# Attention's layer normalisation, in a two-layer decoder on one core: VectorE's apply step becomes a GpSimd shift and a ScalarE ACTIVATE

## The reference

```python
def _layernorm(x, axis=-1, eps=1e-05):
    m = jnp.mean(x, axis=axis, keepdims=True)
    v = jnp.var(x, axis=axis, keepdims=True)
    return (x - m) / jnp.sqrt(v + eps)
...
    x = _layernorm(x + _L0_attn_ref(x, ...), axis=-1)                 # a long convolution
    x = _layernorm(x + _L0_xattn_ref(x, ctx_1024, ...), axis=-1)      # cross attention, 16 heads of 32
    x = _layernorm(x + _L0_ffn_ref(x, ...), axis=-1)
    x = _layernorm(x + _L1_attn_ref(x, ...), axis=-1)                 # retention
    x = _layernorm(x + _L1_xattn_ref(x, ctx_1024, mask, ...), axis=-1)  # cross attention, masked
    x = _layernorm(x + _L1_ffn_ref(x, ...), axis=-1)
```

```python
        scores = jnp.einsum('bhqd,bhkd->bhqk', q, k) / scale
        attn = jax.nn.softmax(scores, axis=-1)
        out = jnp.einsum('bhqk,bhkd->bhqd', attn, v)
        return out @ Wo + bo
```

## Time and profile before

| | |
|---|---|
| median of 3 runs | 2520.98 us (2520.63 to 2522.58) |
| the profiled execution, its own time | 2518.09 us |
| its span, first to last instruction | 2516.3 us |
| mean granted TensorE clock | 0.902 |
| TensorE busy | 2193.9 us, 87% |
| VectorE busy | 1147.9 us, 46% |
| ScalarE busy | 946.2 us, 38% |
| GpSimd busy | 761.2 us, 30% |

### The profile page before, as it was taken

The page is one execution under the profiler, slowest core; times in us unless marked ns, Lnnn a source line. Parts: engine busy times, 40 slices in busy tenths (PEclk is TensorE's granted clock), DMA queues, the critical chain, the costliest instruction groups (busy, mean ns, idle before and its releaser), DMA issues.

```text
span 2516.3 us, 36343 instructions
## 1 busy us (share of the span) xinstructions
PE 2193.9 (87%) x12528; PEld 2014.5 (80%) x12528; DVE 1147.9 (46%) x1742; ACT 946.2 (38%) x1603; POOL 761.2 (30%) x554
## 2 busy tenths in 40 slices
PE   4798889888866889689988889879999999999997
PEld 3687778777755777578777778769999999999996
DVE  7456666566556268446566665554620001100022
ACT  2354545454442244345444545442222223211131
POOL 4333232233243633422133222222222222222222
PEclk9798899898867978789988999869999999999998
DMA  4354455344321100255354454321111121112111
GB/s 152 109 152 111 123 139 138 100 127 127 117 70 30 34 11 0 86 174 146 102 137 112 120 143 134 92 80 46 66 51 59 58 64 61 51 58 67 58 50 43
DMA packets 126422, 226.33 MB, mean 90 GB/s; under 512 B 39896, under 2 KB 77016, under 8 KB 126232
## 3 DMA queue, kind: packets, MB, share of 16 engines
q1 hardware_dynamic: 126360, 225.52, 30.9%
HBM read 169.93 MB, written 55.53 MB: 90 GB/s over the span
## 4 chain that ended last, share of the span: by engine, by line
PE 75%; DVE 10%; issue 6%; POOL 4%; ACT 3%; DMA 1%; SPq 1%; DVEq 0%; POOLq 0%; ACTq 0%
PE psS L310 13%; PE psS L312 12%; PE psS L311 12%; PE psO L1607 6%; PE psJ L310 4%; PE psS L1564 4%; PE psJ L311 4%; PE psJ L312 4%; PE psT L1593 3%; PE psT L310 3%; DVE psS L1129 2%; PE psT L311 2%; PE psT L312 2%; PE psS L1593 2%; DVE x_res L1083 2%
## 5 line engine op out<-in xcount | busy, mean ns | idle before, releaser
L310 PE MATMUL psS<-hid_hi,fw_hi 128*128 128x400 f32 x1152 | 397.9, 345 | 15.3 <-DVE hid_lo L1490 10.6
L312 PE MATMUL psS<-hid_hi,fw_lo 128*128 128x400 f32 x1152 | 400.0, 347 | 0.0
L311 PE MATMUL psS<-hid_lo,fw_hi 128*128 128x400 f32 x1152 | 399.4, 347 | 0.0
L690 POOL TENSOR_TENSOR fw_lo<-raw,fw_hi 128x1024 fp32r<-128x1024 f32 x88 | 216.6, 2461 | 572.5 <-ACT fw_hi L947 572.5
L513 POOL TENSOR_TENSOR pT<-p,pT 128x600 fp32r<-128x600 f32 x112 | 164.9, 1473 | 656.7 <-ACT pT L775 656.7
L1129 DVE TENSOR_REDUCE psS<-psS 100x1 f32<-100x722 f32 x256 | 234.6, 916 | 195.8 <-PE psS L1564 195.4
L1490 DVE TENSOR_TENSOR hid_lo<-h_act,hid_hi 128x800 fp32r<-128x800 f32 x32 | 32.3, 1082 | 555.7 <-ACT hid_hi L1039 555.7
L1564 PE MATMUL psS<-kS,qS 97*100 97x512 f32 (+1 forms) x512 | 165.6, 391 | 119.4 <-DVE psS L1129 81.1
L310 PE MATMUL psJ<-cT_hi,wk_hi 128*128 128x362 f32 (+1 forms) x512 | 189.9, 371 | 62.6 <-POOL cT_lo L506 36.1
L310 PEld LDWEIGHTS psS<-hid_hi,fw_hi 128*128 128x128 f32 x1152 | 217.9, 189 | 16.3 <-issue 11.3
L312 PEld LDWEIGHTS psS<-hid_hi,fw_lo 128*128 128x128 f32 x1152 | 219.2, 190 | 0.0
(11 more groups left out here) (315 smaller groups left out, 4677.6 us busy)
## 6 DMA issues: line engine op xcount, KB each, us to landing
kS<-k_parts SPq DMA_DIRECT2D x384, 180.5 KB
raw<-ffn_dram SPq DMA_DIRECT2D x88, 512.0 KB, 3.5
k_parts<-kst SPq DMA_DIRECT2D x64, 362.0 KB, 3.2
k_parts<-kst SPq DMA_DIRECT2D x64, 360.0 KB, 2.8
ctx_raw<-ctxT_dram SPq DMA_DIRECT2D x32, 361.0 KB, 3.8
ctx_late<-ctxT_dram SPq DMA_DIRECT2D x28, 361.0 KB, 3.8
qS<-q_parts SPq DMA_DIRECT2D x192, 50.0 KB, 2.2
q_parts<-qst SPq DMA_DIRECT2D x16, 400.0 KB, 2.6
```

Of the source, the lines that this page charges most:

```text
L310: nc.tensor.matmul(out, st[0], mv_[0], start=first, stop=False)
L311: nc.tensor.matmul(out, st[0], mv_[1], start=False, stop=False)
L312: return nc.tensor.matmul(out, st[1], mv_[0], start=False, stop=last)
L690: nc.gpsimd.tensor_tensor(fw.lo[:, e, :], raw[:, e, :], fw.hi[:, e, :], ALU.subtract)\
```

## The change

In the 7 batches of each attention layer that follow another one, the apply step of pair 3 is no longer VectorE's. GpSimd computes the shift, -mean x rstd, into `veps`, directly behind the root in pair 1 (`shift`). ScalarE writes x_res = rstd x y + shift with one ACTIVATE (`norm_apply` in its own block), in pair 3, behind the copy of the maxima, and tells `ln_x`. It waits for a new semaphore `A.shift`. The normalisation of each layer's last batch stays on VectorE, and so do all others.

```diff
+            def shift(L, b):
+
+                n = (LN_ATT0, LN_ATT1)[L] + b
+                wait_apart(pool, ln_rstd, n + 1)
+                nc.gpsimd.tensor_scalar(veps[:, 0, :], mv[:, 0, 0:1], rstd[:, 0, :], -1.0, ALU.mult, ALU.mult)\
+                  .then_inc(A.shift, 1)
...
                         if t == 1 and not first:
                             root(base + b - 1, 0)
+                            shift(L, b - 1)
...
+                def norm_apply(b):
+
+                    act.wait_ge(A.shift, b + (NB - 1) * L + 1)
+                    nc.scalar.activation(x_res[:, b, :], y[:, 0, :], ACT.Identity, bias=veps[:, 0, :],
+                                         scale=rstd[:, 0, :]).then_inc(ln_x, 1)
...
-                def batch(b, last):
+                def batch(b, last, first=False):
...
                         if t == 2 and not last:
                             context_hi(L, b + 1, 0)
+                        if t == 3 and not first:
+                            norm_apply(b - 1)
...
-                batch(0, False)
+                batch(0, False, first=True)
...
                         if t == 4:
                             low_parts(b, 2 * t + 1)
-                        if t == 3 and not first:
-                            norm_apply(base + b - 1, 0, y[:, 0, :], b - 1)
```

More of the change, by code:

```diff
@@ L259, in decoder_kernel @@
                          "q_mm q_hi q_lo q_out0 q_out1 qs_in0 qs_in1 qs_in2 qs_in3 s_mm maxed nm_hi nm t_mm rows_set st_mm exped pt_hi lo_even lo_odd pv_mm "
-                         "u_done sums r_done z_done x_done o_sum o_scaled o_biased o_hi o_lo resid_done mask_in mask_done "
+                         "u_done sums r_done z_done x_done o_sum o_scaled o_biased o_hi o_lo resid_done mask_in mask_done shift "
                          "mask_out pads")
```

## The result

| | us |
|---|---|
| before, median of 4 runs beside the change | 2521.2 (2520.63 to 2522.58) |
| after, median of 4 runs | 2432.97 (2430.58 to 2437.87) |
| ratio, 95% interval | 0.9652 (0.9635 to 0.9668) |
| after, profiled execution: own time, span, granted clock | 2434.05, 2432.3, 0.921 |

A forecast was written before the change was run, and what follows sets the result against it. TensorE bounds the kernel, waiting while VectorE's normalisation stands still until GpSimd's run ends. Loops 77.3 less ScalarE's 1.2 gives 76.1 us off 2518.09, 2442; plus 2.9 for the median, 2445 us; range 2429 to 2464.

The forecast's parts named there:

- The loops, 77.3 us: Twelve attention loop cycles, freed of VectorE's held normalisation, fall from 913.85 to 836.6 us.
- The mean of two controls: Each layer's first batch, with no previous batch to normalise, took 69.03 and 70.40 us; 69.7 forecast per loop cycle.
- ScalarE, 0.77 us with 0.1 to spare, a charge of 1.2 us: Pair 3's new ACTIVATE takes 0.77 us, fits before head 8's exponential; 0.1 us a batch charged for lateness.
- GpSimd, nothing: The shift behind pair 1's root takes 0.4 us, covered by 2.74 us of idle time, so costs nothing.
- The last batches, nothing: Each layer's last batch splits no context slices, so VectorE is not held long; 0 gain for both.
- The sum: Whole kernel: 76.1 us off the profiled 2518.09 gives 2442 us; 2.9 us added for the median gives 2445.
- A: Attention cycles: TensorE's clock stays low, only the 5.1 us stalls go; gain 61 us, 2460 us; chance 0.09.
- B: Pair 3: ScalarE's ACTIVATE is held 6.6 us beside GpSimd's run; gain 16 us, 2505 us; chance 0.03.
- C: Attention cycles: TensorE settles at the low clock of 0.54, 59 us slower, 2580 us; chance 0.03.
- D: Key projection stays at 453.3 anyhow, no change, chance 0.02; partial form, a new 3 us wait, 2480 us, 0.03.

The follow-up runs named there:

- e1: Kernel before, with the apply step left on VectorE but moved from pair 3 to pair 5, behind the output sums: 2433.98 us, ratio 0.9659.
- e3: Kernel after, plus an unused VectorE maximum over 100x6144 at the step's old place in the twelve loop batches: 2513.05 us, ratio 0.9968.
- e4: Kernel after, with ScalarE's new apply step done twice, the second waiting for the first: 2438.50 us, ratio 0.9680.
- e5: Kernel after, with pair 3's apply step back on VectorE in the two last batches alone: 2439.46 us, ratio 0.9681.
- e2: Kernel before, with the apply step on VectorE at its old place, cut into pieces of 257 and 255 elements: 2519.99 us, ratio 1.0003.
- e7: Kernel after, with context slice 1's low part moved from GpSimd to VectorE in pair 3 of every batch but the last: 2484.76 us, ratio 0.9858.
- e9: Kernel after, plus an unused VectorE reduction over 100x3072 in the twelve loop batches, half of an earlier 100x6144 block: 2468.03 us, ratio 0.9797.

## Why the prediction was right, and where not

- *The loops, 77.3 us.* Measured 79.3. The mechanism is shown three ways: take the step away (after), move it out of the run (e1), put a stall of the same length back (e3).
- *The mean of two controls.* Right, and for a reason I did not have: the cycles fall into the controls' two kinds.
- *ScalarE, 0.77 us with 0.1 to spare, a charge of 1.2 us.* Measured 0.82 and 0.17 to spare, so the charge should have been about nothing. That lateness arrives whole was too strong (e4: two thirds).
- *GpSimd, nothing.* The idle time ahead of the next low probabilities fell from 2.74 to 2.19 us, so the shift cost 0.55 us, all covered. e1 has neither the shift nor the ACTIVATE, and its loops are only 0.3 us shorter.
- *The last batches, nothing.* This is the term that was mis-sized: 6.5 us by e5, 5.4 of it seen in the trace of layer 1's last batch. I looked at how long VectorE is held and at layer 0's 0.54 us, and passed over layer 1, where the step took 1.72 us. What it cost there was hardly the pause, and mostly the clock at which TensorE worked afterwards. In layer 0 nothing came of it: head 8 of its last batch to head 8 of layer 1's first took 454.4 us before and 454.1 after.
- *The sum.* The profiled execution took 2434.05 us where 2442 was worked out. Of these 8 us, 2.0 are the loops, 1.2 the ScalarE charge and 7.2 the end of layer 1, against 2.7 us lost up to head 8 of layer 0's batch 0 and in layer 1's batch 0: 7.7. The other 4 us up to the medians come from the executions: I added 2.9 us because before's median lies above its profiled execution; after's lies 1.1 below it. Why layer 1's batch 0 ran at 0.90 is open. That the time lies in the range is in part luck: the loops as forecast reached down to 2435 us, the rest down to 2429 was meant for loop cycles at a clock of 1.00, which did not come, and what filled it was the end of layer 1, a term put at nothing.
- *Rivals.* A (clock gives nothing back) is out: 0.96 for 0.91. B (the hold moves) is out: 817 ns. C and D are out with the loops' 834.58 us.

## What to carry to other kernels

When a VectorE operation that should take half a microsecond takes several, look whether it ends just as a GpSimd operation, or a whole uninterrupted run of them, ends. If so, move the step to where VectorE has slack, or hold GpSimd back with a wait at the end of a stage: here the first was worth as much as moving the step to another engine (e1). Price a stall by TensorE's cycle around it, not by its own length: a cycle of the same work without the stall is the best estimate, and a pause of 1.3 us cost more than five in one place. After a bound is gone, follow who released the next wait: here VectorE, then GpSimd and ScalarE's cast at once, which had to be moved together.

## What the hardware showed that was not expected

- In the attention loops VectorE was held until GpSimd's run ended, whatever it had left to do: 6.61 us before for the whole row, 6.47 for half of it (e2), 3.75 for a tensor_tensor beside two GpSimd operations (e7). These ended 0.29, 0.15 and 0.76 us behind the run. Elsewhere a tensor_tensor was let in behind the first of two GpSimd operations (1.53 us, e7), and a reduction from SBUF was not held at all (3.34 us inside the run, e9).
- The clock's part of a stall was nearly a step: 1.4 us a cycle for a delay of 1.8 us, 1.6 for 5.0 (e9, e3), as the rest of each cycle's growth.
- A pause of TensorE of 1.30 us where the kernel after has 0.43 cost 5.4 us in one batch: behind it the granted clock was 0.50, where without it it stayed at 1.00 (e5).
